# Linear attention and a routed mixture of experts on one core: the second expert tile gets operands and a bank of its own, and h is transposed one product later

## The chip, the cores and the metric

The kernel runs on one core of one Trainium2 chip. The metric is device time in microseconds, the median of several runs. TensorE (PE) multiplies matrices, ScalarE (ACT) and VectorE (DVE) work on elements, GpSimd (POOL) does the rest and issues the gathers, SyncE (SP) issues the plain transfers. Each engine has its own instruction stream; semaphores order them against each other.

## What is computed

```python
x = x + attn(layernorm(x))            # x is 2048 x 512, 32 heads of 64, linear attention
# the experts, E = 8, top 2, D = 512, H = 352:
scores = xf @ gate_w.T + gate_b + bias
top_scores, top_idx = top_k(scores, 2)
gates = softmax(top_scores)
h = silu(xf @ w1[e].T + b1[e])        # for the two experts e of each token
y = h @ w2[e].T + b2[e]
x = x + sum(gates[e] * y)
```

## The kernel before

The attention and the routing fill about the first 780 us. From 773 us on the weights of the experts are transposed on TensorE (`w_transpose`, 46 steps, L1882) and split. Every number that enters a product is kept as two halves in the type fp32r, hi and lo, and each product is made of three (`three`, L1614 to L1616: hi*hi, hi*lo, lo*hi).

The tokens are sorted by expert into NS = 39 tiles of 128 rows; a tile belongs to one expert. For tile i the work goes through the engines like this:

- POOL, `gather(i)` (L691): fetches the 128 rows of x by indirect DMA into xg, two buffers in turn. From i = 2 on it waits until gT(i-2) is done.
- PE, `pe_gT(i)` (L1958): four transpositions of xg into the bank pT. It waits for the gather, and until gT_lo(i-1) has read pT.
- ACT, `act_gT(i)` (L1127): gT_hi from pT. It waits until h(i-1) is done, since there is one gT_hi.
- DVE, `dve_gT(i)` (L1564): gT_lo = pT - gT_hi (recorded at L1199, the helper `lo`).
- PE, `pe_h(i)`: twelve products into the first 352 columns of the bank pK, called h(i) below. The weights' address comes from the tile's expert, which `expert(i)` loads from tile_expert into a register (L1992, "value load").
- ACT, `act_h(i)` (L1133): copies h into h_in, of which there is one.
- PE, `pe_hT(i)` (L1976): three transpositions of h_in into pX.
- ACT, `act_silu(i)` (L1141): silu with bias into hT, three instructions; the expert's number is loaded into a register of ACT first (L1150; for tile 0 L1160).
- DVE, `dve_hT(i)`: hT_hi (L1572) and hT_lo (L1199), two buffers each.
- PE, `pe_y(i)`: nine products into the second half of pK, called y(i); the last two tiles use banks of pA.
- DVE, `dve_y(i)` (L1580): y times the gate. POOL, `add_out(i)` (L710): adds the rows to the output by indirect DMA.

The order on TensorE is written by hand. It begins with gT(0), the last two steps of w_transpose, the value loads of tiles 0 and 1, h(0), gT(1), hT(0), h(1), gT(2), hT(1). Then a loop runs over pairs of tiles, for each i: h(i), gT(i+1), y(i-2), hT(i). At the end stand h(38), y(36), hT(38), y(37), y(38). ACT goes, for each i: h_in(i), gT_hi(i+1), value load, silu(i). DVE goes gT_lo(i+1), y(i-2), hT(i). POOL computes a small table (L772 to L785) that says which output additions must wait for each other; it stands between gather(2) and gather(3), and `after_ready` tells that it is done. DVE waits for it ahead of gT_lo(3). In the main loop POOL goes gather(i+5), add_out(i).

Of the kernel before, what the change touches and what calls it, by code (L numbers as in the profile page):

```python
# [47 lines left out]
E = 8  # L48
# [15 lines left out]
def block_kernel(nc, x, Wq, Wk, Wv, Wo, bo, gate_w, gate_b, gbias, w1, b1, w2, b2, out):  # L64
# [5 lines left out]
    def sb(name, cols, at, dt=F32, parts=P):  # L70
        assert at + (2 if dt in (BF16, F16) else 4) * cols <= 229344 - BASE, name
        return nc.alloc_sbuf_tensor_at(name, [parts, cols], dt, offset=BASE + at)
# [142 lines left out]
    gT_lo = sb("gT_lo", D, 186 * KB, F32R)  # L215
    h_in = sb("h_in", H, 188 * KB)
# [7 lines left out]
    with ExitStack() as ctx:  # L224
# [177 lines left out]


# [160 lines left out]
        def _(pool):  # L564
# [121 lines left out]
            def gather(i):  # L686
                if i == 0:
                    pool.wait_ge(ids_ready, 1)
                if i >= 2:
                    pool.wait_ge(gT_put, i - 1)  # L690
                pool.indirect_dma_start(xg[:, i % 2 * D:(i % 2 + 1) * D], None, xn2_dram,  # L691
                                        bass.IndirectOffsetOnAxis(slot_token[:, i:i + 1].bitcast(U32), 0)).then_inc(s_g[i % 2], 16)
# [33 lines left out]
            def tab(ins):  # L726
                tabled[0] += 1
                ins.then_inc(table_step, 1)
                pool.wait_ge(table_step, tabled[0])
# [43 lines left out]
            tab(pool.tensor_copy(add_base[:, :], add_iota[:, 0:NS]))  # L773
            tab(pool.tensor_tensor(same[:, :], padt[:, 1:TW], padt[:, 0:NS], ALU.subtract))
# [12 lines left out]
            for i in range(3, 5):  # L787
                gather(i)
# [10 lines left out]
        def _(act):  # L799
# [294 lines left out]
            def w_hi(k):  # L1094
                act.wait_ge(w_put, k + 1)
                src, rows, dst = w_step(k, w1_hi, w2_hi, w_bank(k))
                nc.scalar.copy(dst, src).then_inc(w_hi_ready, 1)
# [25 lines left out]
            def act_gT(i):  # L1123
                act.wait_ge(gT_put, i + 1)
                if not (isinstance(i, int) and i == 0):
                    act.wait_ge(h_put, i)
                nc.scalar.copy(gT_hi[:, :], pT[:, :]).then_inc(gT_hi_ready, 1)  # L1127

            def act_h(i):
                act.wait_ge(h_put, i + 1)  # L1130
                if not (isinstance(i, int) and i == 0):
                    act.wait_ge(hT_put, i)
                nc.scalar.copy(h_in[:, :], pK[:, 0:H]).then_inc(h_ready, 1)  # L1133
# [11 lines left out]
            def act_tile_e(i, e=None, last=False):  # L1145
                act_h(i)
                if not last:
                    act_gT(i + 1)
                if e is None:
                    e = act.value_load(tile_expert[0:1, ds(i, 1)], min_val=0, max_val=E - 1)  # L1150
                act_silu(i, e)
# [3 lines left out]
            for k in range(WSTEPS - 2, WSTEPS):  # L1155
                w_hi(k)
            act.wait_ge(far_ready, 1)
# [4 lines left out]
            act_tile_e(0, first_expert)  # L1162
            with act.Fori(1, NS - 1) as i:
                act_tile_e(i)
            act_tile_e(NS - 1, last=True)
# [3 lines left out]
        def _(dve):  # L1169
# [28 lines left out]
            def lo(dst, src, hi):  # L1198
                return nc.vector.tensor_tensor(dst, src, f(hi), ALU.subtract)  # L1199
# [364 lines left out]
            def dve_gT(i):  # L1564
                dve.wait_ge(gT_hi_ready, i + 1)
                lo(gT_lo[:, :], pT[:, :], gT_hi[:, :]).then_inc(gT_lo_ready, 1)
# [21 lines left out]
            dve_hT(0, 0)  # L1588
            put_gates()
            dve_gT(2)  # L1590
            dve_hT(1, 1)
            dve.wait_ge(gates_ready, 1)
            dve.wait_ge(after_ready, 1)
            for i in range(2, 4):
                dve_gT(i + 1)
                dve_y(i - 2, i % 2, 0)
                dve_hT(i, i % 2)
            with dve.Fori(2, NS // 2) as h:
                for b in range(2):
                    dve_gT(2 * h + (b + 1))  # L1600
                    dve_y(2 * h + (b - 2), b, 16 * h - 16)
                    dve_hT(2 * h + b, b)
# [9 lines left out]
        def _(pe):  # L1612
# [348 lines left out]
            def pe_h(i, e):  # L1961
                pe.wait_ge(gT_lo_ready, i + 1)
                if not (isinstance(i, int) and i == 0):
                    pe.wait_ge(h_ready, i)
                for n in range(FB):
                    last = three(pK[:, 0:H], two((gT_hi, gT_lo), n * P, P), two((w1_hi, w1_lo), e * H + n * EH, H),
                                 n == 0, n == FB - 1)
                last.then_inc(h_put, 1)
# [26 lines left out]
            for k in range(WSTEPS - 2, WSTEPS):  # L1995
                w_transpose(k)
            pe.wait_ge(experts_ready, 1)
# [4 lines left out]
            pe_gT(1, 1)  # L2002
            pe_hT(0)
            pe_h(1, first_experts[1])
            pe_gT(2, 0)
            pe_hT(1)
            pe.wait_ge(w_lo_ready, len(DVE_STEPS))
            with pe.Fori(1, NS // 2) as h:
                for b in range(2):
                    i = 2 * h + b  # L2010
                    pe_h(i, expert(i))
                    pe_gT(2 * h + (b + 1), 1 - b)
                    pe_y(2 * h + (b - 2), b, expert(2 * h + (b - 2)))
                    pe_hT(i)
            pe_h(NS - 1, expert(NS - 1))
            pe_y(NS - 3, 0, expert(NS - 3))
# [27 lines left out]
```

## Time and profile before

| | us |
|---|---|
| median of 3 runs | 1011.93 (1011.74 to 1012.09) |
| the profiled execution, its time | 1011.67 |
| its span | 1010.0 |
| PE busy | 996.3 (99%) |
| DVE busy | 686.4 (68%) |
| ACT busy | 514.0 (51%) |
| POOL busy | 259.3 (26%) |

The span is that of the profiled execution, from its first to its last instruction; its time holds 1.67 us more that lie around it. All moments below are microseconds from the start of the span. Ends of TensorE's products are modelled and overlap the next one, so one reads starts: from one start to the next is what a product costs.

### The profile page before, as it was taken

To read this page: it belongs to the slowest core of one execution; us is meant where nothing else is said; L and a number is where in the kernel's file an instruction comes from. 1 tells how busy PE (TensorE), PEld (TensorE's weight loads), DVE (VectorE), ACT (ScalarE), POOL (GpSimd) and SP (SyncE) were. 2 spreads that over 40 slices of the span, in tenths; PEclk is the share of its full clock that TensorE was granted. 3 is DMA by queue.
4 is the path that set the end of the run, shared out by engine and by line. 5 is a ranking of instruction groups with operands and counts; after the bars stand their busy time and mean duration, and the time that the engine had idled before them with its cause. 6 is when DMAs were issued, how large, how long until landed. Compare 5 with 4: busy or idle time off the path is not lost.

```text
span 1010.0 us, 17489 instructions
## 1 busy us (share of the span) xinstructions
PE 996.3 (99%) x5029; PEld 840.0 (83%) x5030; DVE 686.4 (68%) x1552; ACT 514.0 (51%) x1324; POOL 259.3 (26%) x413
## 2 busy tenths in 40 slices
PE   8999999999999999999999999999999989999998
PEld 7888888888888888888788888888888879988996
DVE  7888655565666667667877878777887665544544
ACT  4545444454444457755555555555554954343442
POOL 1000000000000002222423233333333645656564
PEclk9999999999999999999999999999999999999999
DMA  7002501000000011343221111111125635555653
GB/s 262 23 21 84 209 27 36 21 21 21 21 22 21 21 63 63 104 173 116 43 53 49 45 42 42 42 42 42 42 73 161 187 119 101 108 102 99 110 107 48
DMA packets 46861, 75.35 MB, mean 75 GB/s; under 512 B 6089, under 2 KB 18554, under 8 KB 46690
## 3 DMA queue, kind: packets, MB, share of 16 engines
q1 hardware_dynamic: 37010, 56.04, 18.0%
q0 software_dynamic: 9808, 18.79, 10.1%
q8 instruction: 21, 0.34, 0.1%
q14 instruction: 22, 0.18, 0.1%
HBM read 53.14 MB, written 23.50 MB: 76 GB/s over the span
## 4 chain that ended last, share of the span: by engine, by line
PE 93%; DVE 3%; ACT 2%; DMA 1%; issue 1%; SPq 0%; POOL 0%; POOLq 0%; DVEq 0%; ACTq 0%
PE pK L1614 16%; PE pK L1616 16%; PE pK L1615 16%; PE pA L1614 6%; PE pA L1616 6%; PE pA L1615 6%; PE pX L1614 6%; PE pX L1616 5%; PE pX L1615 5%; PE pA L1748 3%; PE pT L1958 2%; PE pT L1694 2%; PE pX L1976 1%; PE pA L1882 1%; DVE w_lo L1523 1%; PE pT L1629 1%
## 5 line engine op out<-in xcount | busy, mean ns | idle before, releaser
L965 ACT ACTIVATE qs<-q,nrec 128x64 f32<-128x64 f32 x512 | 129.6, 336 | 88.0 <-DVE nrec L1344 87.9
L586 POOL TENSOR_TENSOR wv_lo<-wv_in,wv_hi 128x512 fp32r<-128x512 f32 x4 | 5.2, 1292 | 403.0 <-ACT wo_hi L886 403.0
L1614 PE MATMUL pA<-k_hi,xn_hi 128*128 128x512 f32 x256 | 101.0, 394 | 0.5 <-DVE k_lo L1219 0.5
L1614 PE MATMUL pK<-wq_hi,xnT_hi 128*128 128x512 f32 x256 | 100.4, 392 | 0.0
L1614 PE MATMUL pK<-wk_hi,xnT_hi 128*128 128x512 f32 (+1 forms) x256 | 100.1, 391 | 0.2 <-DVE xnT_lo L1199 0.2
L1616 PE MATMUL pK<-wq_hi,xnT_lo 128*128 128x512 f32 x256 | 99.9, 390 | 0.0
L1616 PE MATMUL pA<-k_hi,xn_lo 128*128 128x512 f32 x256 | 99.8, 390 | 0.0
L1615 PE MATMUL pK<-wk_lo,xnT_hi 128*128 128x512 f32 (+1 forms) x256 | 99.7, 390 | 0.0
L1615 PE MATMUL pA<-k_lo,xn_hi 128*128 128x512 f32 x256 | 99.7, 389 | 0.0
L1616 PE MATMUL pK<-wk_hi,xnT_lo 128*128 128x512 f32 (+1 forms) x256 | 99.7, 389 | 0.0
L1615 PE MATMUL pK<-wq_lo,xnT_hi 128*128 128x512 f32 x256 | 99.7, 389 | 0.0
L1614 PE MATMUL pX<-m_hi,qsT_hi 128*128 128x512 f32 x240 | 99.0, 413 | 0.0
L1616 PE MATMUL pX<-m_hi,qsT_lo 128*128 128x512 f32 x240 | 94.2, 393 | 0.0
L1615 PE MATMUL pX<-m_lo,qsT_hi 128*128 128x512 f32 x240 | 93.7, 390 | 0.0
L1337 DVE TENSOR_TENSOR qs<-q,ksum 128x512 f32<-128x512 f32 x64 | 51.8, 809 | 55.6 <-ACT q L959 55.6
L710 POOL DMA_INDIRECT out<-y,slot_token x38 | 70.2, 1847 | 65.0 <-DVE y L1580 43.1
L1219 DVE SCALAR_TENSOR_TENSOR k_lo<-pK,k_hi 128x512 fp32r<-128x512 f32 x64 | 44.0, 688 | 56.1 <-ACT k_hi L833 56.1
L827 ACT CAST xn_hi<-xn 128x512 fp32r<-128x512 f32 x64 | 39.8, 622 | 69.3 <-PE pA L1616 69.3
L959 ACT ACTIVATE q<-pK 128x512 f32<-128x512 f32 x64 | 38.2, 597 | 68.2 <-PE pK L1616 68.2
L833 ACT ACTIVATE k_hi<-pK 128x512 fp32r<-128x512 f32 x64 | 38.1, 595 | 66.4 <-PE pK L1616 66.3
L1141 ACT ACTIVATE hT<-pX,b1T 128x128 f32<-128x128 f32 (+1 forms) x117 | 34.1, 363 | 72.0 <-PE pX L1976 72.0
L1199 DVE TENSOR_TENSOR xn_lo<-xn,xn_hi 128x512 fp32r<-128x512 f32 x64 | 44.0, 688 | 27.7 <-ACT xn_hi L827 27.7
(277 smaller groups left out, 2447.7 us busy)
## 6 DMA issues: line engine op xcount, KB each, us to landing
w_in<-in_ffn_w SPq DMA_DIRECT2D x22, 256.0 KB, 3.6
w_in<-in_ffn_w SPq DMA_DIRECT2D x8, 704.0 KB, 7.6
xn<-in_attn_hidden_states SPq DMA_DIRECT2D x16, 256.0 KB, 6.3
wv_in<-in_attn_Wv SPq DMA_DIRECT2D x16, 256.0 KB, 2.8
wo_in<-in_attn_Wo SPq DMA_DIRECT2D x16, 256.0 KB, 3.0
wk_in<-in_attn_Wq SPq DMA_DIRECT2D x4, 1024.0 KB, 5.7
xnT_dram<-xnT SPq DMA_DIRECT2D x4, 1024.0 KB, 11.6
x_in<-in_attn_hidden_states SPq DMA_DIRECT2D x16, 256.0 KB, 2.6
```

What stands on the lines that cost most here:

```text
L710: pool.indirect_dma_start(out, bass.IndirectOffsetOnAxis(slot_token[:, i:i + 1].bitcast(U32), 0), rows, None, bounds_check=T - 1, oob_is_e ...
L827: nc.scalar.copy(xn_hi[:, b * D:(b + 1) * D], xn[:, ds(t * D, D)]).then_inc(xn_hi_ready, 1)
L833: nc.scalar.activation(k_hi[:, b * CW:(b + 1) * CW], pK[:, b * 512:(b + 1) * 512], ACT.Relu).then_inc(k_hi_ready, 1)
L959: nc.scalar.activation(q[:, b * CW:(b + 1) * CW], pK[:, b * 512:(b + 1) * 512], ACT.Relu).then_inc(q_ready, 1)
L965: i = nc.scalar.activation(qs[:, s], q[:, s], ACT.Copy, scale=nrec[:, b * HC + h:b * HC + h + 1])
L1141: last = nc.scalar.activation(hT[0:w, b * P:(b + 1) * P], pX[0:w, b * P:(b + 1) * P], ACT.Silu, bias=b1T[0:w, ds(b * E + e, 1)])
L1199: return nc.vector.tensor_tensor(dst, src, f(hi), ALU.subtract)
L1219: nc.vector.scalar_tensor_tensor(out=k_lo[:, s], in0=pK[:, b * 512:(b + 1) * 512], scalar=0.0, in1=f(k_hi[:, s]), op0=ALU.max, op1=ALU.sub ...
L1337: nc.vector.tensor_tensor(qs[:, b * CW:(b + 1) * CW], q[:, b * CW:(b + 1) * CW], ksum[:, c * CW:(c + 1) * CW], ALU.mult).then_inc(qk_ready, 1)
L1614: nc.tensor.matmul(dst, lhs[0], rhs[0], start=start, stop=False)
L1615: nc.tensor.matmul(dst, lhs[0], rhs[1], start=False, stop=False)
L1616: return nc.tensor.matmul(dst, lhs[1], rhs[0], start=False, stop=stop)
```

## The change

Tile 1 gets operands g1_hi and g1_lo of its own, in memory that y uses later, and its h goes into a free bank of pA. gT(1) moves ahead of the two value loads and of h(0). h(1) comes right behind h(0). hT(i-1) now stands behind h(i), on all engines, where hT(i) stood behind y(i-2). gather(3) moves ahead of most of the table.

```diff
+    g1_hi = sb("g1_hi", D, M0 + 1024, F32R)
+    g1_lo = sb("g1_lo", D, M0 + 3072, F32R)
...
+        h_bank = lambda i: pA[:, 1024:1024 + H] if isinstance(i, int) and i == 1 else pK[:, 0:H]
+        g_of = lambda i: (g1_hi, g1_lo) if isinstance(i, int) and i == 1 else (gT_hi, gT_lo)
...
             tab(pool.tensor_copy(add_base[:, :], add_iota[:, 0:NS]))
+            gather(3)
             tab(pool.tensor_tensor(same[:, :], padt[:, 1:TW], padt[:, 0:NS], ALU.subtract))
...
-            for i in range(3, 5):
-                gather(i)
+            gather(4)
...
-                if not (isinstance(i, int) and i == 0):
+                if not (isinstance(i, int) and i < 2):
                     act.wait_ge(h_put, i)
-                nc.scalar.copy(gT_hi[:, :], pT[:, :]).then_inc(gT_hi_ready, 1)
+                nc.scalar.copy(g_of(i)[0][:, :], pT[:, :]).then_inc(gT_hi_ready, 1)
...
-                nc.scalar.copy(h_in[:, :], pK[:, 0:H]).then_inc(h_ready, 1)
+                nc.scalar.copy(h_in[:, :], h_bank(i)).then_inc(h_ready, 1)
...
+            act_gT(1)
             act.wait_ge(far_ready, 1)
...
-            act_tile_e(0, first_expert)
-            with act.Fori(1, NS - 1) as i:
-                act_tile_e(i)
-            act_tile_e(NS - 1, last=True)
+            act_h(0)
+            act_h(1)
+            act_gT(2)
+            act_silu(0, first_expert)
+            with act.Fori(2, NS - 1) as i:
+                act_h(i)
+                act_gT(i + 1)
+                act_tile_e(i - 1)
+            act_h(NS - 1)
+            act_tile_e(NS - 2)
+            act_tile_e(NS - 1)
...
             dve_gT(1)
-            dve_hT(0, 0)
             put_gates()
             dve_gT(2)
-            dve_hT(1, 1)
+            dve_hT(0, 0)
...
                 for b in range(2):
                     dve_gT(2 * h + (b + 1))
+                    dve_hT(2 * h + (b - 1), 1 - b)
                     dve_y(2 * h + (b - 2), b, 16 * h - 16)
-                    dve_hT(2 * h + b, b)
+            dve_hT(NS - 2, 1)
...
+            pe_gT(1, 1)
             pe.wait_ge(experts_ready, 1)
             first_experts = [expert(i) for i in range(2)]
             pe.wait_ge(w_lo_ready, len(DVE_STEPS) - 2)
             pe.wait_ge(w_act_ready, len(PE_STEPS))
             pe_h(0, first_experts[0])
-            pe_gT(1, 1)
+            pe_h(1, first_experts[1])
             pe_hT(0)
-            pe_h(1, first_experts[1])
             pe_gT(2, 0)
-            pe_hT(1)
...
                     pe_h(i, expert(i))
+                    pe_hT(2 * h + (b - 1))
                     pe_gT(2 * h + (b + 1), 1 - b)
                     pe_y(2 * h + (b - 2), b, expert(2 * h + (b - 2)))
-                    pe_hT(i)
             pe_h(NS - 1, expert(NS - 1))
+            pe_hT(NS - 2)
             pe_y(NS - 3, 0, expert(NS - 3))
             pe_hT(NS - 1)
             pe_y(NS - 2, 1, expert(NS - 2))
```

## Rows read from the trace of the kernel before

**Rows 1.** Windows, two stretches: busy time of each engine, PEclk, DMA.

```profile
814.46:823.93 9.47, 6.34 (x38) 5.34 (x39) 4.92 (x11) 4.42 (x13) 5.99 (x17) 1.00 0.20 58
833.53:995.99 162.46, 162.46 (x955) 146.73 (x953) 80.39 (x136) 64.58 (x170) 95.68 (x66) 1.00 0.56 101
```

**Rows 2.** Timeline of PE, the first tiles: gT(0), h(0), gT(1), h(2).

```profile
812.93 0.66 PE L1958 MATMUL pT<-ident,xg 128*128 128x128 f32 x4
...
815.72 0.42 PE L1614 MATMUL pK<-w_hi,gT_hi 128*128 x1 [1.26 <-DVE gT_lo L1199]
...
817.74 0.60 PE L1958 MATMUL pT<-ident,xg 128*128 128x128 f32 x4
...
823.93 0.42 PE L1614 MATMUL pK<-w_hi,gT_hi 128*128 x1 [0.83 <-DVE gT_lo L1199]
```

**Rows 3.** Timeline of PE, in the loop: gT, y, hT, next h.

```profile
830.76 0.60 PE L1958 MATMUL pT<-ident,xg 128*128 128x128 f32 x4
831.12 0.47 PE L1614 MATMUL pK<-w_hi,hT_hi 128*128 x1
...
833.29 0.49 PE L1976 MATMUL pX<-ident,h_in 128*128 128x128 f32 x3
833.53 0.41 PE L1614 MATMUL pK<-w_hi,gT_hi 128*128 x1
```

**Rows 4.** Timeline of DVE: gT_lo(0), the last memset, gT_lo(2).

```profile
814.78 0.68 DVE L1199 TENSOR_TENSOR gT_lo<-pT,gT_hi 128x512 fp32r<-128x512 f32 x1
...
816.99 0.17 DVE L1558 MEMSET hT<- 1x128 f32 x1
...
823.10 0.69 DVE L1199 TENSOR_TENSOR gT_lo<-pT,gT_hi 128x512 fp32r<-128x512 f32 x1 [1.96 <-ACT gT_hi L1127]
```

**Rows 5.** Timeline of ACT: h_in(1), gT_hi(2).

```profile
822.04 0.45 ACT L1133 COPY h_in<-pK 128x352 f32<-128x352 f32 x1 [1.99 <-PE pK L1616]
822.48 0.59 ACT L1127 CAST gT_hi<-pT 128x512 fp32r<-128x512 f32 x1
```

**Rows 6.** Value loads L1992 by stretch, and tile_expert: ns min/median/max, first, last start.

```profile
L1992 PEldq TENSOR_LOAD <-tile_expert x1: 490/490/490, 813.0 to 813.0; - x1
...
L1992 PEldq TENSOR_LOAD <-tile_expert x1: 308/308/308, 813.9 to 813.9; - x1
...
L1992 PEldq SEQ_ASSERT  x1: 18/18/18, 814.4 to 814.4; - x1
...
L765 POOL TENSOR_SCALAR tile_expert<-padt x1: 321/321/321, 807.0 to 807.0; 128x40 int32<-128x40 f32 x1
```

**Rows 7.** Timeline of POOL: gather(1), first and last moved-past table operation.

```profile
809.82 0.94 POOL L691 DMA_INDIRECT xg<-xn_dram,slot_token  x1 [0.31 <-issue]
...
815.43 0.25 POOL L774 TENSOR_TENSOR same<-padt 128x39 f32<-128x39 f32 x1
...
819.27 0.22 POOL L785 CAST add_after<-same 128x39 int32<-128x39 f32 x1
```

**Rows 8.** Tile xg, 805 to 835 us: from a gather's issue to landing.

```profile
DMA to landing us min/median/max: 3.2/3.7/4.4
```

**Rows 9.** Timeline of PE, the end: y(36), hT(38), y(38).

```profile
997.98 0.39 PE L1614 MATMUL pK<-w_hi,hT_hi 128*128 x1
...
1000.07 0.49 PE L1976 MATMUL pX<-ident,h_in 128*128 128x128 f32 x3
...
1002.69 0.49 PE L1614 MATMUL pA<-w_hi,hT_hi 128*128 x1
```

**Rows 10.** Timeline of ACT, the end: h_in(38), silu(38).

```profile
998.18 0.45 ACT L1133 COPY h_in<-pK 128x352 f32<-128x352 f32 x1 [0.93 <-PE pK L1616]
1000.69 0.87 ACT L1141 ACTIVATE hT<-pX,b1T 128x128 f32<-128x128 f32 x3 [2.06 <-PE pX L1976]
```

**Rows 11.** Line L1150, 996 to 1002 us: the check behind ACT's last value load.

```profile
L1150 ACTq SEQ_ASSERT  x1: 18/18/18, 998.7 to 998.7; - x1
```

**Rows 12.** Timeline of POOL, the end: the last addition to the output.

```profile
1006.69 1.55 POOL L710 DMA_INDIRECT out<-y_last,slot_token  x1 [0.85 <-DMA out<-y,slot_token]
```

More of the change, by code:

```diff
@@ L1143, in act_silu, with act_tile_e @@
                 last.then_inc(hT_ready, 1)
[L1145 to L1151, printed above, removed]
+            def act_tile_e(i):
+                act_silu(i, act.value_load(tile_expert[0:1, ds(i, 1)], min_val=0, max_val=E - 1))
             act.wait_ge(w_put, W1T + 3 * (E - 1))
@@ L1565, in dve_gT @@
                 dve.wait_ge(gT_hi_ready, i + 1)
-                lo(gT_lo[:, :], pT[:, :], gT_hi[:, :]).then_inc(gT_lo_ready, 1)
+                lo(g_of(i)[1][:, :], pT[:, :], g_of(i)[0][:, :]).then_inc(gT_lo_ready, 1)
             def dve_hT(i, b):
@@ L1595, in _ @@
                 dve_gT(i + 1)
+                dve_hT(i - 1, 1 - i % 2)
                 dve_y(i - 2, i % 2, 0)
-                dve_hT(i, i % 2)
             with dve.Fori(2, NS // 2) as h:
@@ L1962, in pe_h @@
                 pe.wait_ge(gT_lo_ready, i + 1)
-                if not (isinstance(i, int) and i == 0):
+                if not (isinstance(i, int) and i < 2):
                     pe.wait_ge(h_ready, i)
                 for n in range(FB):
-                    last = three(pK[:, 0:H], two((gT_hi, gT_lo), n * P, P), two((w1_hi, w1_lo), e * H + n * EH, H),
+                    last = three(h_bank(i), two(g_of(i), n * P, P), two((w1_hi, w1_lo), e * H + n * EH, H),
                                  n == 0, n == FB - 1)
```

## The prediction

> **What bounds the kernel now.** I read three things: busy time by stretch, the order of TensorE's instructions at the start, in the middle and at the end of the expert stage, and what ACT and DVE do beside it. Two kinds of stretch must be told apart. From 833.53 to 995.99 us TensorE is busy for 162.46 of 162.46 us [rows 1]: 34 tiles, 4.78 us each. There a new order of the products can win nothing but what the instructions themselves cost. From 814.46 to 823.93 us it is busy for 6.34 of 9.47 us [rows 1]: it waits for the split operands of tiles 0, 1 and 2, longest before h(0), where the idle time is 1.26 us [rows 2]. The granted clock is 1.00 in both stretches [rows 1]. The third place is the end, where the last tiles have nothing to cover them. So the change is decided between 815 and 824 us and behind 996 us.
>
> **The start, step by step.** DVE ends gT_lo(0) at 814.78 + 0.68 = 815.46 [rows 4]. Before, h(0) follows at 815.72 [rows 2], 0.26 later. Now gT(1) stands in front; it must wait for the same event, because gT_lo(0) still reads pT. A transposition has no address to compute, so I let it start 0.05 later, at 815.51. It holds TensorE for 0.36 us (830.76 to 831.12) [rows 3]. Its gather was issued at 809.82 and gathers land in 3.2 to 4.4 us, by 814.2 [rows 7, 8]: no wait.
>
> The next step is the one that decides, I think. The two value loads of `first_experts` stood in front of the wait for gT_lo(0). They ran from 813.0, beside gT(0) of 812.93, to the last check at 814.4 [rows 2, 6]: 1.4 us, all of it before 815.46, at no cost. In the new order they stand behind gT(1), whose wait ends at 815.46. That TensorE's queue gets no further than a waiting instruction, the loads show: the tile that they read is written at 807.0, yet the first begins at 813.0, just when gT(0) gets its rows [rows 2, 6]. So they now begin at 815.6 and end at 817.0; the wait and address steps cost the same 0.26 as before, and h(0) starts at 817.25 instead of 815.72. The cover is gone but for gT(1)'s 0.36 us. Bounds: the loads last 490 and 308 ns [rows 6]; with both at 308 the pair is 0.2 us shorter. Hidden altogether, h(0) starts at 815.87 (rival 1).
> The Trainium skill (DMA: Bandwidth & Descriptors, Latency and other measured facts) gives a tensor_load a floor of about 600 ns. The rows of this trace lie below it (308 and 490 ns); as an estimate by that floor the pair would take 0.4 us more and the sum below would end 0.4 us higher.
>
> h(0) takes 2.02 us (815.72 to 817.74) [rows 2]: h(1) can start at 819.27. Its operands: gT_hi(1) is done by 816.8; DVE's last memset ends at 816.99 + 0.17 = 817.16 and gT_lo takes 0.69 [rows 4]: ready at 817.85. So the spare place and the spare bank do what they are there for, and h(1) waits for nothing. A product's first step behind transpositions is 0.08 us longer (y takes 2.17 us there [rows 3], 2.09 behind a product [rows 9]); h(1) stands behind h(0) and takes 1.94. hT(0) starts at 821.21, gT(2) 0.33 later at 821.54.
> h(2) isn't helped by the spare places. It needs gT_lo(2); act_h(1) stands before act_gT(2) and waits until hT(0) has read h_in. hT(0) ends at 821.21 + 0.49 = 821.70 [rows 3], the copy starts at 821.74, gT_hi(2) follows 0.44 later [rows 5], gT_lo(2) 0.62 after that [rows 4, 5], and h(2) 0.83 after that (823.10 to 823.93) [rows 2, 4]: 823.63. gT(2) itself ends at 821.54 + 0.60 = 822.14, just ahead of gT_hi(2) at 822.18. **Gain at h(2): 0.30 us** (823.93 before).
>
> POOL's queue: gather(3) now stands before twelve table operations (815.43 to 819.49) [rows 7] and waits for gT(1). It goes at 816.2, takes about 1.0 us and lands by 821; gT(3) wants it at 826. The table ends near 821.4, gather(4) goes at 822.2, wanted after 830. DVE waits for that table ahead of gT_lo(3), at 826. All of that is hidden by 4 us or more. On ACT the first load and the tanh stand between gT_hi(1) and h_in(0), wanted at 819.5: hidden. The memory of y that serves as g1 isn't written before y(0), about 828.
>
> **The loop.** Each tile has the same instructions. hT(i-1) and gT(i+1) now stand together, seven transpositions of 0.11 us. Each block of them gives 0.08 us of its last one back as the next product's longer first step, so one block of seven costs what two blocks do: I take 0. The bounds are 0 and a gain of 0.01 us a tile, 0.4 us in all. Does another chain become long enough to matter? From the start of h(i), h and hT end at 1.94 + 0.49 = 2.43, gT at 1.94 + 0.33 + 0.60 = 2.87; gT_hi(i+1) starts at 2.91, gT_lo at 3.53, h(i+1) could start at 4.36 [rows 2 to 5]. It starts at 4.78: 0.42 us of margin, where before it was 0.68 (830.76 + 0.60 + 0.04 + 0.62 + 0.83 = 832.85 against 833.53 [rows 3]). So the period stays at 4.78.
>
> **The end.** The deferred hT now stands in front of the last products. Before, y(36) ends at 1000.07 [rows 9], 176.14 us after the start of h(2). In the new order hT(37) lies in between too: 0.24 + 0.08 = 0.32 us [rows 3]. y(36) ends at 823.63 + 176.14 + 0.32 = 1000.09: the gain is used up. Then y(37) needs hT_lo(37), whose silu stands behind h_in(38) and a value load on ACT. hT(37) starts at 1000.09 - 2.09 - 0.32 = 997.68 and ends at 998.17; h_in(38) starts at 998.21. Its load's last check comes 0.5 us later (998.18 to 998.7 before) [rows 10, 11], and the silu starts about 0.2 us on, at 998.89. It lasts 0.87 us, and from a silu's end to the product that needs it are 1.13 us (1001.56 to 1002.69) [rows 9, 10]: y(37) starts at 1000.89; before, it followed hT(38) and its 0.25 us, at 1000.32. Then 2.17 us: y(38) at 1003.06 instead of 1002.69 [rows 9], 0.37 late. But y(38) started out of a wait, with the longer first step, and now saves 0.08. hT(38) and its split are done by 1002.8. What follows y(38), to the last issue at 1006.69 [rows 12], is unchanged. **Sum: +0.29 us**; for the merged transpositions I take off 0.1.
> Against the profiled execution (span 1010.0 us, time 1011.67 us) that gives 1010.2 and 1011.86. The median of the runs is 1011.93, 0.26 above the profiled time; from the median the forecast is **1012.1 us**, no change. A measurement of this kernel can tell about 0.2%, 2.0 us.
>
> **Rivals.**
> 1. *The loads are hidden.* If TensorE's queue lets them pass the wait, h(0) starts at 815.87, h(1) at 817.99 (by gT_lo(1)), and h(2) 1.28 us earlier than in my sum; all behind it moves along: 1010.8 us. For it: nothing needs the loads' order. Against it: the first load at 813.0. Chance 0.12; by my bound still no change.
> 2. *The loop's chain becomes the bound* (slower). h_in's copy now waits for a transposition behind h, and gT_hi waits for the copy. If this chain is x us longer than I make it, each of 36 tiles pays x - 0.42. From x = 0.48 on it is over 2 us; at 0.52 it is 36 x 0.1 = 3.6 us: 1015.7 us. For it: a third of the margin goes. Against it: its links are rows of this trace. Chance 0.04.
> 3. *The tail costs nothing.* If silu(37) isn't held by the copy and the load, only y(36)'s place counts: 1011.9 us. Chance 0.1, no change either.
> 4. *A large gain*: transpositions in a row cost 0.05 us a tile less, 1.8 us, on top of rival 1: 1009.0 us. Against it: rows at the same 0.11 in both blocks. Chance 0.02. And *the clock falls* in one of the gaps, none over 1.5 us; 1.26 us left it at 1.00 [rows 1, 2]: a loss of some 2 us, chance 0.02.
>
> **The numbers.** The forecast has 0.7, the rivals 0.12, 0.04, 0.1 and 0.04 for the last two. The likeliest case spans 1011.6 to 1012.7. The range takes in rivals 1 and 3 and the bounds of the loads and the silu: 1010.8 to 1013.0. Faster by over 0.2%: 0.03; within it: 0.92; slower: 0.05.
>
> **What would show it.** gT(1) at 815.5, then 1.1 us of idle time with the two loads in it; h(1) right behind h(0); h(2) at 823.6; a period of 4.78 without idle time; h(38) 0.3 us early; a gap of about 0.5 us before y(37). Wrong would be: idle time before h in the loop, an h(0) before 816.5, or a gap before gT(3) for its rows.

## The result, and the profile after

The changed kernel takes 1013.44 us in the median of 22 runs (1012.86 to 1016.28), the kernel before 1012.03 (22 runs, 1011.60 to 1012.81). The ratio is 1.0016, with a 95% interval of 1.001 to 1.0022. By the bound of 0.2% this is no change, as forecast. But the interval leaves out 1: the kernel is 1.4 us slower where 0.2 was forecast, and it lies above the range of 1010.8 to 1013.0.

Where did the 1.4 us go? I cut the expert stage at four moments that every trace shows: D is the end of gT_lo(0) on DVE, then come the starts of h(2) and of h(38) on TensorE, and last the start of POOL's last addition. The table holds the profiled executions; the forecast's column is worked out from the prediction's own moments.

| us | before | forecast | after |
|---|---|---|---|
| D | 815.46 | 815.46 | 815.98 |
| D to h(2) | 8.47 | 8.17 | 8.29 |
| h(2) to h(38) | 172.06 | 172.11 | 172.65 |
| h(38) to the last addition | 10.70 | 11.24 | 11.47 |
| sum behind D | 191.23 | 191.52 | 192.41 |

Behind D the change costs 192.41 - 191.23 = 1.18 us. D itself varies with the execution: over the 14 traces of this study it lies between 815.32 and 816.05, in no order by what the kernels change.

The start, in the timeline of TensorE after, beside [rows 2]:

```profile
813.43 0.66 PE L1966 MATMUL pT<-ident,xg 128*128 128x128 f32 x4
...
816.12 0.63 PE L1966 MATMUL pT<-ident,xg 128*128 128x128 f32 x4 [1.16 <-DVE gT_lo L1207]
817.91 0.42 PE L1622 MATMUL pK<-w_hi,gT_hi 128*128 x1 [1.16 <-DVE w_lo L1531]
...
819.93 0.32 PE L1622 MATMUL pA<-w_hi,g_hi 128*128 x1
...
821.86 0.49 PE L1984 MATMUL pX<-ident,h_in 128*128 128x128 f32 x3
822.18 0.60 PE L1966 MATMUL pT<-ident,xg 128*128 128x128 f32 x4
824.27 0.42 PE L1622 MATMUL pK<-w_hi,gT_hi 128*128 x1 [1.49 <-DVE gT_lo L1207]
```

And the value loads (L2000) between 811 and 820 us, beside [rows 6]; the columns are ns min/median/max, then the first and last start. PEldq is TensorE's queue; each load is followed by register operations and by a check of the value (SEQ_ASSERT):

```profile
L2000 PEldq TENSOR_LOAD <-tile_expert x2: 309/401/493, 816.1 to 817.0; - x2
L2000 PEldq FUSED_REGOPS  x2: 156/160/165, 816.7 to 817.4; - x2
L2000 PEldq SEQ_ASSERT  x2: 18/23/28, 816.9 to 817.6; - x2
```

gT(1) at 816.12 is 0.14 behind D. Both loads begin only then, and the last check is at 817.6, just ahead of h(0) at 817.91. The trace names w_lo as what ended h(0)'s wait, but the part of that work that h(0) waits for was done at 815.37, ahead of D; a reader who believed the name would miss the loads. h(1) stands right behind h(0), and it has no idle time: the spare place and bank work. The loads last 309 and 493 ns, as before. The Trainium skill (DMA: Bandwidth & Descriptors, Latency and other measured facts) has about 600 ns as the floor of a tensor_load; both rows lie below it. The last loads of the stage are longer here: 687 ns ahead of y(37), below.

The loop, by windows of the 34 tiles (busy time of PE, PEld, DVE, ACT and POOL, PEclk, DMA), beside [rows 1]:

```profile
833.87:996.30 162.43, 162.43 (x952) 148.41 (x951) 78.31 (x136) 62.26 (x169) 87.40 (x67) 1.00 0.56 101
```

TensorE is full here, as before, and at the same granted clock. So the 0.6 us more of the loop (172.65 - 172.06) is work that takes longer, not waiting. It sits in single tiles. Two neighbours, h(36) and h(37), in the timeline of TensorE after:

```profile
987.34 0.33 PE L1622 MATMUL pK<-w_hi,gT_hi 128*128 x1
987.50 0.32 PE L1623 MATMUL pK<-w_lo,gT_hi 128*128 x1
...
989.24 0.49 PE L1984 MATMUL pX<-ident,h_in 128*128 128x128 f32 x3
...
992.09 0.33 PE L1622 MATMUL pK<-w_hi,gT_hi 128*128 x1
992.26 0.32 PE L1623 MATMUL pK<-w_lo,gT_hi 128*128 x1
992.42 0.33 PE L1624 MATMUL pK<-w_hi,gT_lo 128*128 x1
...
994.08 0.49 PE L1984 MATMUL pX<-ident,h_in 128*128 128x128 f32 x3
```

The first h takes 989.24 - 987.34 = 1.90 us, the second 994.08 - 992.09 = 1.99. In the kernel before, h stands behind transpositions and takes 1.99 to 2.02 in every tile from 3 on, the longer first step included. After, h takes 1.90 to 1.95 in 28 of the 36 tiles from 3 on, and 1.99 in eight.

The end of TensorE after (beside [rows 9]), of ACT, of DVE and of POOL, and the value load of TensorE in the same stretch:

```profile
998.83 0.49 PE L1984 MATMUL pX<-ident,h_in 128*128 128x128 f32 x3
999.08 0.48 PE L1622 MATMUL pK<-w_hi,hT_hi 128*128 x1
...
1001.26 0.49 PE L1984 MATMUL pX<-ident,h_in 128*128 128x128 f32 x3
1002.30 0.49 PE L1622 MATMUL pA<-w_hi,hT_hi 128*128 x1 [0.54 <-DVE hT_lo L1207]
...
1004.49 0.40 PE L1622 MATMUL pA<-w_hi,hT_hi 128*128 x1
```

```profile
999.41 0.45 ACT L1138 COPY h_in<-pK 128x352 f32<-128x352 f32 x1 [2.70 <-PE pX L1984]
1000.13 0.87 ACT L1146 ACTIVATE hT<-pX,b1T 128x128 f32<-128x128 f32 x3 [0.27 <-issue]
```

```profile
1001.43 0.56 DVE L1207 TENSOR_TENSOR hT_lo<-hT,hT_hi 128x384 fp32r<-128x384 f32 x1
```

```profile
1008.39 1.55 POOL L715 DMA_INDIRECT out<-y_last,slot_token  x1 [0.55 <-issue]
```

```profile
L2000 PEldq TENSOR_LOAD <-tile_expert x1: 687/687/687, 1001.2 to 1001.2; - x1
L2000 PEldq SEQ_ASSERT  x1: 18/18/18, 1002.1 to 1002.1; - x1
```

From y(36) to y(37) are now 1002.30 - 999.08 = 3.22 us, before 1000.32 - 997.98 = 2.34. The trace names hT_lo for the wait ahead of y(37). hT_lo(37) ends at 1001.43 + 0.56 = 1001.99, but y(37)'s own value load comes later still: TensorE's queue stood at hT(38), which waits for silu(37) (it ends at 1001.00), so the load begins only at 1001.2 and its check stands at 1002.1. It is the start's mechanism once more, a load behind a wait.

### The profile page after: what moved, and what is told of

Its sections match the earlier page's. It is cut to its first block, busy times and chain, and to the rows that moved or that the text cites. A ratio compares the mean times of both kernels' runs of the same rounds, so it can differ in the third digit from the quotient of the medians.

```text
span 1011.6 us, 17465 instructions
## 1 busy us (share of the span) xinstructions
PE 996.1 (98%) x5029; PEld 842.4 (83%) x5030; DVE 684.3 (68%) x1552; ACT 511.9 (51%) x1324; POOL 250.7 (25%) x413
## 4 chain that ended last, share of the span: by engine, by line
PE 93%; DVE 3%; ACT 2%; issue 1%; DMA 1%; POOL 0%; SPq 0%; ACTq 0%; DVEq 0%; POOLq 0%
PE pK L1622 16%; PE pK L1624 16%; PE pK L1623 16%; PE pA L1622 6%; PE pA L1624 6%; PE pA L1623 6%; PE pX L1622 6%; PE pX L1624 5%; PE pX L1623 5%; PE pA L1756 3%; PE pT L1966 2%; PE pT L1702 2%; PE pX L1984 1%; DVE w_lo L1531 1%; PE pA L1890 1%
## 5 line engine op out<-in xcount | busy, mean ns | idle before, releaser
L1207 DVE TENSOR_TENSOR gT_lo<-pT,gT_hi 128x512 fp32r<-128x512 f32 x38 | 26.3, 691 | 78.4 <-ACT gT_hi L1132 78.4
L715 POOL DMA_INDIRECT out<-y,slot_token x38 | 60.1, 1581 | 75.2 <-DVE y L1588 49.5
L1138 ACT COPY h_in<-pK 128x352 f32<-128x352 f32 x38 | 17.2, 453 | 104.4 <-PE pX L1984 101.7
```

The costliest lines, as they stand in the source:

```text
L715: pool.indirect_dma_start(out, bass.IndirectOffsetOnAxis(slot_token[:, i:i + 1].bitcast(U32), 0), rows, None, bounds_check=T - 1, oob_is_e ...
```

## The experiments

Each experiment was timed beside the kernel before on the same chip, whose median was 1012.04 to 1012.07 us. The last table of this section holds the stretches of all of them. The cuts of code show TensorE's part; where the order of the tiles changes, ACT and DVE follow it.

**a0: the changed kernel again; b0: the kernel before again.** No edit. They show how far the stretches repeat.

> The changed kernel once more, to see which part of its 1.7 us against the kernel before lies in its own stage. I cut the profiled execution at four marks: the start of gT(0), of h(2), of h(38), and the last addition to the output. The two traces so far give 11.00 / 172.06 / 10.70 us for before and 10.84 / 172.65 / 11.47 for the changed one, and gT(0) started at 812.93 and 813.43. Theory: the 0.50 us ahead of gT(0) is chance of one execution (nothing differs there), the stretches are the change's: again 10.8 / 172.6 / 11.5 within 0.1, and gT(0) anywhere from 812.5 to 814. Rival: the later gT(0) belongs to the changed program (longer code, other placement): again 813.4 or later. Time 1013.4.

> The kernel before once more, with a profile. Its parts should repeat within 0.1 us: from the end of gT_lo(0) to h(2) 8.47 us, h(2) to h(38) 172.06, h(38) to the last addition 10.70. The end of gT_lo(0) itself lay at 815.46 before and at 816.07, 816.15, 815.45, 815.74 and 815.61 in five kernels that differ only behind it. Theory: that is chance of one execution, it falls anywhere between 815.3 and 816.2. Rival: it is later in longer programs: 815.46 again. And in no execution does TensorE's clock fall between 814 and 826 (theory of the clock), so all times lie below 1013.

a0: 1013.67 us (11 runs, ratio 1.0022, 1.0013 to 1.0031). b0: 1011.93 (11 runs, ratio 1.0, 0.9991 to 1.0009). Behind D both repeat each stretch of the first trace of their kernel within 0.07 us. In b0 gT(0) starts at 813.46, as late as in the changed kernel, where [rows 2] have 812.93. So a late start isn't the change's doing.

**e1: the value loads ahead of gT(1).**

```diff
-            pe_gT(1, 1)
             pe.wait_ge(experts_ready, 1)
             first_experts = [expert(i) for i in range(2)]
+            pe_gT(1, 1)
```

> The changed kernel with its two value loads on TensorE moved back ahead of gT(1). Theory (TensorE's queue stands still at gT(1)'s wait, so the loads behind it are in the open): gT(1) at the same place, h(0) about 0.35 us behind gT(1)'s start instead of 1.79, h(1) then bound by gT_lo(1), h(2) earlier by about 1.3 us: gT(0) to h(2) 9.6 us instead of 10.84. Time 1.2 to 1.3 us less, about 1012.2. Rival (the wait before h(0) is for the weights' split, as the releaser in the trace says, w_lo): h(0) stays 1.8 us behind gT(1), time unchanged.

1011.99 us (11 runs, 1011.45 to 1014.05), ratio 1.0001 (0.9992 to 1.001). TensorE in its timeline:

```profile
815.50 0.63 PE L1966 MATMUL pT<-ident,xg 128*128 128x128 f32 x4 [1.46 <-DVE gT_lo L1207]
815.89 0.40 PE L1622 MATMUL pK<-w_hi,gT_hi 128*128 x1
```

h(0) follows gT(1) by 0.39 us instead of 1.79, and D to h(2) is 7.00 instead of 8.29: 1.29 us less. The step on the loads holds, and rival 1's size for hidden loads (1.28) with it.

**e2: the deferral alone**, on all engines, in the kernel before; no spare places, the old start.

```diff
                     pe_h(i, expert(i))
+                    pe_hT(2 * h + (b - 1))
                     pe_gT(2 * h + (b + 1), 1 - b)
                     pe_y(2 * h + (b - 2), b, expert(2 * h + (b - 2)))
-                    pe_hT(i)
...
             pe_h(NS - 1, expert(NS - 1))
+            pe_hT(NS - 2)
```

> The kernel before with only the second part of the change: hT(i-1) behind h(i), from hT(1) on, in the loop and at the end, on all engines; no spare places, gT(1) and the loads where they were. Theory: the loss of the loop and of the end comes from the deferral alone: gT(0) to h(2) 11.0 as before; h(2) to h(38) 172.6 (0.5 more than before: some h take 1.99 us instead of 1.91); from h(38) to the last addition 11.5 instead of 10.7. In all 1.3 us more than before: 1013.3. Rival: the loop's slower tiles come of the shifted phase against the transfers, which the start sets: then the loop is 172.1 and the loss only 0.8.

1013.48 us (11 runs), ratio 1.0014 (1.0005 to 1.0023). Loop 172.66, end 11.64: the deferral alone costs 0.60 in the loop and 0.94 at the end. The end is 0.18 longer than in a0 though silu(37) and hT_lo(37) come at the same place; y(37)'s value load has its check later here (1002.3, h(38) at 996.89; in the changed kernel 1002.1 and 996.92). e3 and e4 have long loads there too, 842 and 905 ns, and ends of 11.64 and 11.78.

**e3: DVE takes y(i-2) ahead of hT(i-1)**, as in the kernel before; all else changed. It asks whether DVE's order makes the slow tiles.

```diff
-                    dve_hT(2 * h + (b - 1), 1 - b)
                     dve_y(2 * h + (b - 2), b, 16 * h - 16)
+                    dve_hT(2 * h + (b - 1), 1 - b)
```

> The changed kernel with DVE's order in the loop from tile 2 on as it was before: y(i-2) ahead of hT(i-1). Theory A: the 0.5 us in the loop come from what DVE does while TensorE streams h (in the changed kernel hT_lo and y lie under h, and under 8 of 35 tiles h takes 1.99 us instead of 1.91): another order on DVE moves them, h is 1.91 in most tiles and the stretch from h(2) to h(38) falls from 172.65 to about 172.2. Theory B: it comes from the transfers (gathers and additions) meeting h: the stretch stays at 172.5 to 172.8. The rest as in the changed kernel; time 1013.0 by A, 1013.4 by B.

The loop takes 172.65 us again, with the same eight slow tiles: the theory that DVE's order does it falls. The 172.65 lies where the second theory, the transfers, had it, but they don't pick the tiles in the changed kernel's trace: under the eight slow h they move 27 to 149 GB/s, under the others 61 to 160. But the kernel came out at 1014.63 (9 runs, 1013.12 to 1015.29), ratio 1.0023 (1.0013 to 1.0033), and its trace shows why. Windows of the first tiles (PEclk is the third number from the right):

```profile
816.00:818.40 2.40, 1.24 (x8) 1.00 (x7) 1.86 (x6) 0.72 (x2) 1.26 (x2) 0.96 0.17 70
818.40:821.60 3.20, 3.20 (x12) 3.20 (x12) 0.00 (x0) 0.45 (x1) 2.47 (x9) 0.50 0.29 87
821.60:825.00 3.40, 2.27 (x16) 2.01 (x15) 0.47 (x1) 1.47 (x5) 0.78 (x3) 1.00 0.01 2
```

```profile
815.66 0.63 PE L1966 MATMUL pT<-ident,xg 128*128 128x128 f32 x4 [1.18 <-DVE gT_lo L1207]
817.45 0.42 PE L1622 MATMUL pK<-w_hi,gT_hi 128*128 x1 [1.16 <-DVE w_lo L1531]
...
818.74 0.49 PE L1622 MATMUL pK<-w_hi,gT_hi 128*128 x1
819.04 0.49 PE L1623 MATMUL pK<-w_lo,gT_hi 128*128 x1
```

From 818.4 to 821.6 us the granted clock is 0.50, which is 1.2 GHz instead of 2.4. A product steps at 0.29 to 0.30 us instead of 0.16, and TensorE does 12 products in the 3.2 us. Ahead of the fall it idled for 1.18 us, did gT(1), idled for 1.16 us and did half of h(0). D to h(2) is 9.84 instead of 8.29: 1.55 us lost. In the changed kernel's own trace the same stretch holds at 1.00; but 6 of its 22 executions lie at 1014.2 or above, at mean clocks of 0.995 to 0.998, as do 5 of a0's 11 and 6 of e3's 9 (one of these at 0.999), while none of the kernel before lies above 1013.1. The mean clock alone proves little, since executions of the kernel before have 0.998 too; the fall itself is seen in the traces of e3 and e9.

**e4: one transposition more between y(i-2) and h(i)**, into an unused bank. It asks whether the slow tiles come from h standing right behind y.

```diff
                     pe_y(2 * h + (b - 2), b, expert(2 * h + (b - 2)))
+                    nc.tensor.transpose(pA[:, 1536:1536 + P], ident[:, :], ident[:, :])
```

> The changed kernel with one transposition of the identity more in the loop, behind y(i-2), ahead of the next h; its result is read by nothing. In five traces of the deferred order the same 8 tiles (6, 9, 16, 18, 24, 26, 34, 37) stream h at 0.167 us a product, the others at 0.155 to 0.162; none does in the kernel before, where transpositions stand ahead of every h. Theory C: the slow step comes of h standing directly behind y; with a transposition between no tile is slow, and the stretch from h(2) to h(38) is 172.1 + 36 x 0.109 = 176.0 us. Rival D: it comes of what the other engines and the transfers do beside h, which this leaves nearly where it was: still about 8 tiles of 1.99 + 0.08, and 172.65 + 3.9 = 176.6 us.

1017.06 us (2 runs), ratio 1.005 (1.0032 to 1.0069); the loop takes 176.42. There are slow tiles still, but six others: 7, 9, 17, 25, 33 and 35, with h at 2.07 to 2.08 beside 1.99 to 2.02. The 176.6 of rival D comes nearest. So h right behind y isn't what the slow step needs; what stands around h moves it to other tiles.

**e5: e1 with the old end** (hT(37) ahead of h(38)), the loop deferred.

```diff
+            pe_hT(NS - 2)
             pe_h(NS - 1, expert(NS - 1))
-            pe_hT(NS - 2)
```

> e1 (the value loads ahead of gT(1)) with the end as it was before: hT(37) behind y(35), ahead of h(38), on PE, ACT and DVE. Theory: the deferral costs 0.77 us at the end (11.47 against 10.70 us from h(38) to the last addition), of which about 0.24 is hT(37) itself, done later, the rest a wait before y(37) for hT_lo(37). Now hT(37) lies ahead of h(38) (the loop's stretch to h(38) grows by about 0.33 us to 173.0) and the end is 10.7: in all 0.45 us less than e1: 1011.5. Rival: hT(37) has to wait there for silu(36), which stands behind two copies and a load on ACT: the stretch to h(38) grows by up to 0.8 us and nothing is won.

1012.35 us (11 runs), ratio 1.0004 (0.9995 to 1.0013). The end is 10.72 again, but a wait has appeared ahead of h(38). TensorE's timeline, and its value loads from 995 to 997 us:

```profile
995.54 0.49 PE L1984 MATMUL pX<-ident,h_in 128*128 128x128 f32 x3
996.86 0.42 PE L1622 MATMUL pK<-w_hi,gT_hi 128*128 x1 [0.83 <-issue]
```

```profile
L2000 PEldq TENSOR_LOAD <-tile_expert x1: 796/796/796, 995.5 to 995.5; - x1
L2000 PEldq SEQ_ASSERT  x1: 18/18/18, 996.6 to 996.6; - x1
```

h(2) to h(38) takes 174.00, 1.35 us more. The rival had hT(37) wait for silu(36), whose place it needs. silu(36) ends at 995.32, and hT(37) starts at 995.54 with no idle time of TensorE ahead of it. But until then TensorE's queue stood at that wait, and behind it comes the value load for h(38): it begins at 995.5, takes 796 ns, and its check stands at 996.6, 0.26 ahead of h(38). So the 0.83 us are the loads' mechanism again. What the old end would give with this load ahead of hT(37), no run here shows.

**e6: spare places and e1's start, with the old loop and the old end.** hT(1) gets a bank of its own, so that it can follow gT(2).

```diff
+        hT_bank = lambda i: pA[:, 1536:2048] if isinstance(i, int) and i == 1 else pX[:, :]
...
             pe_hT(0)
             pe_gT(2, 0)
+            pe_hT(1)
...
                     pe_h(i, expert(i))
-                    pe_hT(2 * h + (b - 1))
                     pe_gT(2 * h + (b + 1), 1 - b)
                     pe_y(2 * h + (b - 2), b, expert(2 * h + (b - 2)))
+                    pe_hT(i)
```

> Only the start of the change: spare places and spare bank for tile 1, gT(1) ahead of h(0), gather(3) earlier, the value loads ahead of gT(1) as in e1; hT(1) goes behind gT(2) into a bank of its own (so that it needn't wait for silu(0)), and from h(2) on loop and end are those of the kernel before. Theory: the start's gain stays whole: gT_lo(0) to h(2) 6.9 us as in e1 (8.47 before), h(2) to h(38) 172.1, end 10.7: 1.5 us less than before: 1010.5. Rival: h(2)'s operands or hT(2) wait for silu(1), which now lies behind silu(0) on ACT between gT_hi(2) and h_in(2): up to 0.9 us of idle time ahead of y(0) or h(3), total 1011.4.

1010.31 us (11 runs, 1010.02 to 1010.76), ratio 0.9984 (0.9975 to 0.9993): faster than the kernel before by 1.7 us, and near the 1010.5 that was expected. D to h(2) is 6.99, the loop 172.14 without a slow tile, the end 10.70.

**e7: the idle time of the changed kernel filled** with 27 transpositions of the identity, whose results nobody reads, around gT(1) and behind gT(2).

```diff
+            for n in range(8):
+                nc.tensor.transpose(pX[:, 0:P], ident[:, :], ident[:, :])
             pe_gT(1, 1)
+            for n in range(9):
+                nc.tensor.transpose(pX[:, 0:P], ident[:, :], ident[:, :])
...
             pe_gT(2, 0)
+            for n in range(10):
+                nc.tensor.transpose(pA[:, 1536:1536 + P], ident[:, :], ident[:, :])
```

> The changed kernel with transpositions of the identity in its idle time (8 before gT(1), 9 between gT(1) and the value loads, 10 behind gT(2)), written to banks that nobody reads then. Theory (in some executions the granted clock falls to half in the stage's first tiles, as in e3's trace from 818.4 to 821.6 us, because TensorE idles there for 1.2, 1.2 and 1.5 us close together): the busy engine keeps its clock, no execution lies a whole microsecond above the others, and the times bunch at 1013.3; the changed kernel's own were 1012.9 to 1013.9 in 16 of 22 executions and 1014.2 to 1016.3 in the other 6. Rival: the high times have another cause (a transfer, the state of the chip): again about a quarter of the executions at 1014.2 or more. The fillers delay nothing by more than 0.2 us: each group is shorter than the gap that it stands in.

1012.93 us (11 runs), ratio 1.001 (1.0001 to 1.0019). The three waits shrink to 0.19, 0.23 and 0.39 us, D to h(2) is 8.35, and ten of the eleven executions lie between 1012.78 and 1013.45. The eleventh, 1014.15, has a mean clock of 1.000, so nothing shows a fall in it. Of the changed kernel's 33 executions (22, and a0's 11) eleven lie at 1014.2 or above, here none of 11. The median is 0.5 us lower, but the clock explains little of that: the changed kernel's 16 executions below 1014.2 have a median of 1013.37, still 0.44 above e7's, and behind D the two traces are alike (192.47 and 192.41). The rest lies ahead of D (815.35 and 815.98) and isn't explained.

**e8: gT(i+1) ahead of hT(i-1) in the loop.**

```diff
                     pe_h(i, expert(i))
-                    pe_hT(2 * h + (b - 1))
                     pe_gT(2 * h + (b + 1), 1 - b)
+                    pe_hT(2 * h + (b - 1))
```

> The changed kernel with gT(i+1) ahead of hT(i-1) in the loop. Both orders have seven transpositions between h and y, and h stands directly behind y. Theory: the slow step of h (0.167 us a product) is TensorE's own and goes by the time at which h's first product meets the stream ahead of it; e4 moved it to the tiles 7, 9, 17, 25, 33 and 35, always tiles of the experts 1, 3, 5, 7. Nothing just ahead of h changes here, so the same 8 tiles as in the changed kernel are slow, 172.65 us. Rival: it is the overlap with ACT's and DVE's reads, which now come 0.2 to 0.3 us earlier: other tiles, or another number of them, 172.1 to 173.0.

1016.49 us (4 runs, 1015.27 to 1017.90), ratio 1.0048 (1.0033 to 1.0063). The loop takes 174.91 us, outside what any theory had given. Its timeline shows a limit that none had named, here ahead of h(7), in the timeline with the weight loads (PEld):

```profile
845.91 0.49 PE L1984 MATMUL pX<-ident,h_in 128*128 128x128 f32 x3
...
846.49 0.45 ACT L1138 COPY h_in<-pK 128x352 f32<-128x352 f32 x1 [3.02 <-PE pX L1984]
846.84 0.59 ACT L1132 CAST gT_hi<-pT 128x512 fp32r<-128x512 f32 x1
...
847.47 0.69 DVE L1207 TENSOR_TENSOR gT_lo<-pT,gT_hi 128x512 fp32r<-128x512 f32 x1 [1.98 <-ACT gT_hi L1132]
...
848.30 0.19 PEld L1622 LDWEIGHTS pK<-w_hi,gT_hi 128*128 128x128 f32 x1 [0.25 <-issue]
848.33 0.40 PE L1622 MATMUL pK<-w_hi,gT_hi 128*128 x1
...
848.57 0.32 PE L1623 MATMUL pK<-w_lo,gT_hi 128*128 x1
```

hT comes 0.43 us later, so h_in, gT_hi and gT_lo do too. gT_lo ends at 847.47 + 0.69 = 848.16, the weights of h are loaded at 848.30 and its first product steps at 848.33 without idle time. But its next one steps at 848.57, 0.24 later instead of 0.16, and its weights came just in time and no longer ahead: about 0.07 us a tile, 34 x 0.07 = 2.4 us, near the 2.26 that the loop lost. That the weights are the reason is read from this order of events; no run moves them alone. This is the chain of rival 2 at the very point where its margin ends. In the changed kernel gT_lo ends at 990.83 + 0.69 = 991.52, 0.57 ahead of h(37) at 992.09; less the 0.14 from gT_lo's end to the weights here, a margin of 0.43, where the forecast had 0.42. The slow tiles are others here too, six of them (5, 9, 19, 25, 27 and 37), though nothing just ahead of h has changed: neither "the same 8" nor 172.1 to 173.0 came true.

**e9: ACT's value load for tile 37 ahead of h_in(38).**

```diff
+            last_expert = act.value_load(tile_expert[0:1, NS - 2:NS - 1], min_val=0, max_val=E - 1)
             act_h(NS - 1)
-            act_tile_e(NS - 2)
+            act_silu(NS - 2, last_expert)
```

> The changed kernel with ACT's value load for silu(37) ahead of its wait for h(38). Theory: the end is bound by the chain hT(37), h_in(38), load, silu(37), hT_lo(37), y(37); the copy takes until 0.45 us after its start and the load until 0.72, so the early load saves 0.25 us: from h(38) to the last addition 11.2 instead of 11.47, y(37) 5.1 us behind h(38) instead of 5.38. Rival: silu(37) starts no earlier, since ACT takes the address step only behind the copy: 11.4. In time 1013.1 to 1013.3, too little to be told from the time alone.

1013.89 us (10 runs), ratio 1.0017 (1.0007 to 1.0026). The end is 10.97, 0.50 shorter:

```profile
1000.98 0.45 ACT L1138 COPY h_in<-pK 128x352 f32<-128x352 f32 x1 [2.70 <-PE pX L1985]
1001.33 0.88 ACT L1146 ACTIVATE hT<-pX,b1T 128x128 f32<-128x128 f32 x3
```

The silu follows the copy by 0.35 us instead of 0.72, so hT_lo(37) comes 0.37 earlier. y(37) comes 0.54 earlier, 4.84 instead of 5.38 behind h(38), and has 0.01 of idle time left. The other 0.17 are TensorE's own load for y(37): it takes 300 ns here instead of 687 and is done before hT_lo(37). The median shows nothing of the gain. In this trace the clock fell in the start too (0.62 and 0.52 in the windows from 818 to 820 and 820 to 822 us; D to h(2) 9.82), and 8 of the 10 executions have mean clocks of 0.997 or 0.998.

**e10: e6 with gT(2) between h(0) and h(1)**, and tiles 2 and 3 written out, with hT(1) behind h(2). The cut of code is against e6 and leaves out tile 3.

```diff
             pe_h(0, first_experts[0])
+            pe_gT(2, 0)
             pe_h(1, first_experts[1])
             pe_hT(0)
-            pe_gT(2, 0)
-            pe_hT(1)
...
+            pe_h(2, expert(2))
+            pe_hT(1)
+            pe_gT(3, 1)
+            pe_y(0, 0, first_experts[0])
+            pe_hT(2)
...
```

> e6 (only the start, old loop and end) with the first tiles ordered one step further: h(0), gT(2), h(1), hT(0), h(2), hT(1), gT(3), y(0), hT(2); on ACT h_in(0), gT_hi(2), silu(0), h_in(1). Theory: h(2) waited in e6 for gT_hi(2) behind h_in(1) behind hT(0), an order and not a need; with gT(2) behind h(0) its operands are ready before h(1) ends, and h(2) starts right behind hT(0), about 5.2 us after gT_lo(0) ends instead of 6.99; hT(1) then follows h(2), 0.33 us. Net 1.4 us less than e6: 1008.9. The end (10.70) as in e6. Rival: y(0) or gT(3) waits for silu(0), for its rows or for POOL's table, since all is earlier by 1.7 us now: the stretch from h(2) to h(38) then grows by that, and 1 us or less is won: 1009.5 or more.

1009.73 us (11 runs, 1009.16 to 1010.61), ratio 0.9978 (0.9969 to 0.9987): by the medians 2.3 us faster than the kernel before, 3.7 faster than the changed one. From D to h(3) it takes 10.79 us, e6 11.87, so 1.08 us are won. 1.4 was forecast; by the medians it is 0.6, so the rival's size (1 us or less, 1009.5 or more) fits better. e6 idles for 0.16 and 0.78 us in this stretch; here one wait is left:

```profile
820.66 0.49 PE L1989 MATMUL pX<-ident,h_in 128*128 128x128 f32 x3
820.90 0.40 PE L1627 MATMUL pK<-w_hi,gT_hi 128*128 x1
...
825.77 0.49 PE L1989 MATMUL pX<-ident,h_in 128*128 128x128 f32 x3
826.48 0.42 PE L1627 MATMUL pK<-w_hi,gT_hi 128*128 x1 [0.21 <-issue]
```

```profile
L2005 PEldq TENSOR_LOAD <-tile_expert x1: 302/302/302, 825.6 to 825.6; - x1
```

This is none of the three waits that the rival named. hT(2) waits for silu(1), which ends at 825.46, and the value load for h(3) stands behind it: from 825.6 to a check at 826.2, then h(3) at 826.48.

All stretches, in us, of the profiled executions:

| | D | D to h(2) | h(2) to h(38) | to last addition | median of runs |
|---|---|---|---|---|---|
| b0 | 815.53 | 8.47 | 172.13 | 10.70 | 1011.93 |
| a0 | 816.05 | 8.29 | 172.65 | 11.46 | 1013.67 |
| e1 | 815.36 | 7.00 | 172.65 | 11.46 | 1011.99 |
| e2 | 815.75 | 8.48 | 172.66 | 11.64 | 1013.48 |
| e3 | 815.52 | 9.84 | 172.65 | 11.64 | 1014.63 |
| e4 | 815.44 | 8.29 | 176.42 | 11.78 | 1017.06 |
| e5 | 815.87 | 6.99 | 174.00 | 10.72 | 1012.35 |
| e6 | 815.32 | 6.99 | 172.14 | 10.70 | 1010.31 |
| e7 | 815.35 | 8.35 | 172.65 | 11.47 | 1012.93 |
| e8 | 815.64 | 8.25 | 174.91 | 11.38 | 1016.49 |
| e9 | 816.00 | 9.82 | 172.67 | 10.97 | 1013.89 |

e10's order of the first tiles is another, so only its end (10.70) stands beside these; D is 815.69.

## Why the prediction was right in kind and off in size

The kind held: the start wins a little, the loop stays full, the end gives it back. The size was off by terms that all point to slower. The step that failed is the loop, which the prediction put at nothing and which costs 0.6 us; the second is the end, 0.54 us in the forecast and 0.77 measured.

1. *The loads* were right. gT(1), 1.79 us, h(0) (forecast 1.74); e1 takes them out and wins 1.29. They are what makes the start's gain 0.18 instead of 1.47 us.
2. *h(1) without a wait, h(2) bound by gT_lo(2)*: right. h(0) to h(1) 2.02, to hT(0) 1.93, to h(2) 2.41 us (forecast 2.02, 1.94 and 2.42). The start's miss of 0.12 is the 0.14 from D to gT(1), for which I had 0.05, and the 0.05 at the loads.
3. *The loop* is the term that failed most: "one block of seven costs what two blocks do: I take 0". The chain's part of this step was right: the margin is 0.43. But the loop is 0.54 us over the forecast, and 0.64 with the 0.1 that the prediction took off for the merged transpositions. In the tiles of normal speed the new order is a little cheaper, inside my bounds: h(36) to h(37) takes 4.75 us, and 4.78 before. But eight tiles (6, 9, 16, 18, 24, 26, 34, 37) step at 0.167 us a product instead of 0.155 to 0.162, which is 0.08 us a tile, 0.6 in all. They are the same in every trace with the deferral and y behind gT (after, a0, e1, e2, e3, e5, e7, e9), and there are none with the old loop (before, b0, e6, e10). That the deferral brings them is shown by e2 and e6; why they are slow is open (below). My bounds for this term, 0 and a gain, left out a loss, since I had read them from the average of the same products.
4. *The end*: the forecast cost is 0.54, the measured one 0.77. The mechanism named, a copy and a value load ahead of silu(37), is there: with ACT's load out of the way (e9) the silu starts 0.37 earlier. What was mis-sized: hT(37) to y(37) takes 1002.30 - 998.83 = 3.47 us, for which I had 3.21. Of the 0.26 over, 0.09 lie ahead of the silu and 0.17 behind it, since I took the 1.13 us of [rows 9, 10] from silu to product and it was 1002.30 - 1001.00 = 1.30. These 0.17 have a cause that the prediction left out: y(37) needs a value load of TensorE too, and in the new order it stands behind hT(38)'s wait for silu(37). Where hT_lo(37) does bind y(37), in e9, it starts 0.14 behind its end (1003.20 to 1003.34); so it could have started at 1001.99 + 0.14 = 1002.13, and it starts behind the load's check, at 1002.30. The prediction had found this mechanism at the start and didn't ask for it at the end. e9, where the load is done in time, is 0.17 shorter at just this place.
5. *The clock*: rival 4's second half, chance 0.02, happened in some executions. I argued that 1.26 us of idle time had left the clock at 1.00 and that no new wait would be over 1.5 us. But I looked at each wait by itself. The change makes two close together, 1.16 and 1.16 us with only gT(1) between, and in some executions the clock falls to half in h(0) and h(1), ahead of the third wait (1.49). A fall costs 1.5 us in the two traces that show one (e3, e9); the executions at 1016.3 lost about twice that, and no trace shows how. In the changed kernel and a0 eleven of 33 executions lie at 1014.2 or above. With one wait ahead of h(0), of 1.63 us (e2) or 1.46 (e1), three of 22 lie as far above their median (0.8 us), the highest, at a mean clock of 0.998, by 2.1 us in e1; so a single wait seems to do it more rarely, but the traces of e1 and e2 show no fall. e7 fills the waits with work that nobody needs, and no execution shows a fall. In the median it is little: the 16 of 22 executions below 1014.2 have 1013.37, 0.07 less than all.

The sum: 0.29 forecast behind D, and 0.12 + 0.54 + 0.23 more, makes 1.18, as measured. The rest of the median's 1.41, some 0.2, is the executions with a fallen clock (0.07) and what lies ahead of D, which differs between executions; these runs don't divide that further.

What stays open is the slow step of h. The starts of the products in the trace, in ns from one to the next (worked out from the timeline's records of the changed kernel):

```
tile 8   163 158 158 162 155 159 157 162 155 159 158 163
tile 9   165 162 164 166 167 167 166 167 167 166 167 161
tile 10  164 158 158 161 155 159 158 162 155 159 157 164
```

The same instructions fall into one of two rhythms, and tile 9 slides from the first into the second. All eight tiles lie in the stretches of the loop where the kernel before has h at 1.99 and not at 2.02 us, as do the six of e4 and the six of e8. A tile's expert sets the address of its weights, so the address may have a part in it; no run varies it. The order around h moves the slow step to other tiles (e4, e8), DVE's order doesn't (e3), nor does the moment of the start (e1, e7). Which mechanism it is, and whether it could be foreseen from a trace of before, no run here settles.

## What to carry to other kernels

A register load in an engine's queue is free while it stands ahead of a wait that is longer than it. Right behind a wait it is in the open, and the name that the trace gives the idle time doesn't tell of it. Before an instruction that waits is moved, look at which loads stand behind it in the new order, at every place of the program: here two loads ate 1.3 of 1.5 us at the start, one held y(37) at the end, one made 0.83 us in e5 and one is what e10 still waits for. Splitting a change pays: the spare places, with the loads ahead of gT(1), were good for 1.7 us (e6, e10 for 2.3), the deferral that came with them cost 1.4 (e2). An order that is "the same instructions in a full engine" still has a tail, where deferred work has no cover (0.77 us here), and it can shift the speed of the products themselves (0.6 us here). And waits are better looked at together than one by one: the clock fell behind two of 1.2 us close to each other.

## What the runs showed of the hardware that was not expected

- Products of the same shape (352 columns, same granted clock of 1.00) ran at 0.158 to 0.162 or at 0.167 us a step, tile by tile, the same tiles in eight traces and other ones where the order around them was another (e4, e8).
- TensorE's queue didn't start a value load while the transposition ahead of it waited: the load began within 0.2 us of the end of the wait in the changed kernel (816.1, 1001.2), in e5 (995.5) and in e10 (825.6). Such a load took 300 to 905 ns.
- The granted clock fell to 0.50 for some 3.2 us (e3, 818.4 to 821.6), after waits of 1.18 and 1.16 us with 0.6 us of work between. In the changed kernel's own trace it held at 1.00 with waits of 1.16 and 1.16.
- Where the weights arrived just in time (e8), the first product stepped at 0.24 instead of 0.16 us, with no idle time of TensorE in the trace.
- With ACT's value load ahead of the copy (e9), the silu began 0.35 instead of 0.72 us behind the copy's start, inside the copy's own duration of 0.45.
